# A third picked tile in layers 2 and 3 of a graph network on one core

## Chip, core and metric

The kernel runs on one of the eight cores of one Trainium2 chip. The metric is device time in microseconds of one execution. Short names stand for the units: PE (TensorE matmuls; its weight loads are shown as PEld), DVE (VectorE), ACT (ScalarE), POOL (GpSimd) and SP (SyncE, which here only issues transfers).

## What is computed

A graph of N = 5000 nodes with D = 64 features and E = 165000 edges, sorted by destination. After a layer norm and an encoder, four layers of this run one after the other:

```python
m = relu(x[src] + ea) + EPS            # ea = edge_attr @ eencW + eencb, the same in all layers
logits = m * t
e = exp(logits - segment_max(logits, dst)[dst])
agg = segment_sum(m * e / segment_sum(e, dst)[dst], dst)
h = relu(ln((agg + x) @ W1 + b1)) @ W2 + b2
```

Layers 1 to 3 add h to the running x and take relu(ln(x)) as the next layer's input. A last stage (another layer norm, a weighted sum over edges by source, written as scatters with accumulation) follows.

## The kernel before

**Windows.** The edge list is cut in two halves, h = 0 and 1, that lie on partitions 0 to 63 and 64 to 127 once features are on partitions. A layer goes through 52 full windows of 2 x 1536 edges (FULLW = 52, K = 12 columns of 128 edges for each half) and four of half the size (LAST). Buffers are double, indexed b. The full windows are in a hardware loop of two windows a turn, and every engine has its own program for it; the order on each engine is the order of the text below.

**The gather x[src].** POOL issues one indirect DMA for each column and half (L826, from the node table h_tab in DRAM into xg): 24 a window in layer 0. In later layers some (column, half) pairs, called tiles here, are not gathered but picked by PE: `is_hot` leaves out the tiles with 2*(K-1-k)+h < HOT[l]. With HOT = [0, 2, 2, 2] these are both halves of column 11, and 22 gathers remain in layers 1 to 3. A window's gathers go out only when DVE has copied its index list into idx (L1159), which DVE does at the start of the window two before, once ACT has finished zl of that window (l_ok).

**Picking a tile.** A one-hot matrix of 125 x (40 x 128) fp8 values (`hot[n]`) says which node each of the 128 edges wants. `select` (L910 to L918) multiplies it with `hb`, the node table split into three bf16 parts side by side (192 columns), in 40 matmuls that add up in a PSUM bank. ACT copies the sums to hx (L1066, one copy for each pair of tiles: ROUNDS), and PE's `forward` adds the three parts into the window's PSUM (L893). The matrices of both tiles are made in layer 0, one comparison on DVE each (L1203, `make_hot`; MADE_IN says in which layer tile n is made), stored by SP to DRAM (`keep_hot`, L734), and loaded again in layers 1 to 3 (`load_hot`, L729). There is one buffer for each tile, so SP issues the load for window w when PE has finished that tile's matmuls of window w-1, tile after tile.

**A window on the engines, layers 1 to 3.** PE: forward of window w+1 (L901 transposes of the gathered tiles, L893), back of w (L933, 24 transposes), then select of w+2. ACT: for w+1 keep (L1028), u (L1031, three pieces) and zl (L1035, signals l_ok), then emptying of w to st_all (L1050, six), exponentials (L1057, L1058), the features of w+2 into PSUM (L1042), and the picked rows of w+2 (L1066). DVE: L1159, then four scans (L1166, L1167, L1180, L1184) with small steps between, then make_hot where the layer makes matrices. SP: features ea (L662) and run penalties rp (L651) of w+2, load_hot of w+2, store of st_all (L706), zeros (L711), keep_hot and load_columns (L718) of a made tile.

**Between the layers.** POOL gathers the last row of each node's run from sums (L851), and PE, ACT and DVE do the node part in 11 chunks. As a chunk of h_cur is ready (h_ok), SP stores it to h_tab (`store_nodes`, L714). The next layer's gathers wait for all 11 (tab_out). After layer 3 nothing gathers from these rows; the last stage writes h_tab anew (L1465).

Of the kernel before, what the change touches and what calls it, by code (L numbers as in the profile page):

```python
# [32 lines left out]
N, D, E, L = 5000, 64, 165000, 4  # L33
# [29 lines left out]
NCH = len(NODE_SIZES)  # L63
# [6 lines left out]
XT = 5  # L70
ROWS = EPAD // W
ROWS_REAL = E // W
HOT = [0, 2, 2, 2]
MADE_IN = [0, 0]
NHOT = len(MADE_IN)
ROUNDS = [-(-n // 2) for n in HOT]
PN = N // NT
# [15 lines left out]
def gnn(nc, x, src, dst, edge_attr, edge_weight, encW, encb, eencW, eencb, W1, b1, lnG, lnB, W2, b2,  # L93
# [18 lines left out]
    with ExitStack() as whole:  # L112
# [3 lines left out]
        def sem(name):  # L116
            return whole.enter_context(nc.semaphore(name))
# [372 lines left out]
        with ExitStack() as c:  # L490
# [53 lines left out]
            with ExitStack() as lists_room:  # L544
# [26 lines left out]
            x_ok, xsum_ok, xroot_ok, ha_ok, h_ok, tab_out = (  # L571
                sem(n) for n in ("x_ok", "xsum_ok", "xroot_ok", "ha_ok", "h_ok", "tab_out"))
# [14 lines left out]
            FULL_PAIRS = FULLW // 2  # L587
            SPLIT = [l + 1 < L and HOT[l + 1] > 0 for l in range(L)]
            SPLIT_ROOMS = [(rx.rearrange("p (t d) -> p t d", d=D), slice(0, W // D)),
                           (turn.rearrange("p (t d) -> p t d", d=D), slice(W // D, NT))]  # L590

            def xg_window(l, gr):
                return 16 * (2 * GT - (HOT[l] if gr == NG - 1 else 0))

# [6 lines left out]
            def is_hot(l, k, h, gt):  # L601
                return gt == GT and 2 * (K - 1 - k) + h < HOT[l]

            def made(l):
                return [n for n in range(NHOT) if MADE_IN[n] == l]

# [3 lines left out]
            def in_count(l, w):  # L610
                return 16 * (FULLW * sum(HOT[0:l]) + HOT[l] * (w + 1))

# [3 lines left out]
            def ps_count(l, w, n):  # L616
                return FULLW * sum(HOT[0:l]) + HOT[l] * w + n + 1

# [13 lines left out]
            with nc.Block() as block:  # L632
                @block.sync
                def _(sp):
# [8 lines left out]
                    def keep_features(g, b, gt=GT):  # L643
                        sp.wait_ge(zenc_sb, NG * (g + 1))
                        sp.dma_start(feat_v[g, :, :, 0:gt * P], at[b][:, :, 0:gt * P]).then_inc(feat_out[b], 16)
# [8 lines left out]
                    def load(g, w, b, first):  # L654
                        sp.wait_ge(z_ps, NG * g + NG - NG * 2 + Z0)
                        if first:
                            for h in range(2):
                                piece = bass.ds(h * HALF + w * W, W)
                                sp.dma_start(ea[b][:, h, :, :], edge_attr[piece, :].rearrange("(p k) f -> p k f", k=K)
                                             ).then_inc(ea_in[b], 16)  # L660
                        else:
                            sp.dma_start(turned[b][:, :, :], feat_v[w]).then_inc(ea_in[b], 16)  # L662
                        load_penalties(g, w, b)
# [32 lines left out]
                    def store_small(g, s, b):  # L696
                        sp.wait_ge(back_sb, BU * (g + 1) + BS0)
                        begin = FULLW * W + s * W // 2
                        sp.dma_start(halves[:, begin:begin + W // 2, :].rearrange("h (p k) c -> p h (k c)", k=K // 2),
                                     st[b][:, :, 0:K // 2, :].rearrange("p h k c -> p h (k c)")).then_inc(st_out[b], 16)  # L700
# [3 lines left out]
                    def store(g, w, b):  # L704
                        sp.wait_ge(back_sb, BU * (g + 1) + BS0)
                        sp.dma_start(sums_v[w], st[b].rearrange("p h k c -> p h (k c)")).then_inc(st_out[b], 16)  # L706
# [3 lines left out]
                    def clear(g):  # L710
                        sp.dma_start(head_pieces[g], zeros[:, :]).then_inc(heads_zero, 16)  # L711
# [5 lines left out]
                    def load_columns(n, w, b):  # L717
                        sp.dma_start(hot_srcB[n][b][:, :], hot_rows[n // 2, n % 2, w].partition_broadcast(P)  # L718
                                     ).then_inc(hot_src_in[b], 16)
# [3 lines left out]
                    def load_hot(l, w):  # L723
                        for n in range(HOT[l]):
                            if isinstance(w, int) and w == 0 and n == 0:
                                sp.wait_ge(hot_out, out_count(l, 0))
                            if not (isinstance(w, int) and w == 0):
                                sp.wait_ge(hot_ps, ps_count(l, w - 1, n))
                            sp.dma_start(hot_words[n][0:PN, :], hot_tab[n][w]).then_inc(hot_in, 16)  # L729

                    def keep_hot(l, w, b, more):
                        for j, n in enumerate(made(l)):
                            sp.wait_ge(hot_made, made_count(l, w, j))
                            sp.dma_start(hot_tab[n][w], hot_words[n][0:PN, :]).then_inc(hot_out, 16)  # L734
                            if more:
                                load_columns(n, w + 2, b)
# [17 lines left out]
                    def layer(l, first):  # L754
                        for n in made(l):
                            for b in range(2):
                                load_columns(n, b, b)
                        for w in range(2):
                            load_hot(l, w)
                        with sp.Fori(0, FULL_PAIRS - 1) as i:  # L760
                            for b in range(2):
                                load(l * LW + 2 * i + 2 + b, 2 * i + 2 + b, b, first)
                                if first:
                                    keep_features(2 * i + b, b)
                                load_hot(l, 2 * i + 2 + b)
                                store(l * LW + 2 * i + b, 2 * i + b, b)
                                clear(l * NW + 2 * i + b)
                                keep_hot(l, 2 * i + b, b, True)
                        for b in range(2):
                            load_small(l * LW + FULLW + b, b, b, first)  # L770
                            if first:
                                keep_features(FULLW - 2 + b, b)
                            store(l * LW + FULLW - 2 + b, FULLW - 2 + b, b)
                            clear(l * NW + FULLW - 2 + b)
                            keep_hot(l, FULLW - 2 + b, b, False)
                        for b in range(2):
                            load_small(l * LW + FULLW + 2 + b, 2 + b, b, first)
                            if first:
                                keep_features(FULLW + b, b, GT // 2)
                            store_small(l * LW + FULLW + b, b, b)  # L780
                            clear(l * NW + FULLW + b)
                        for b in range(2):
                            if first:
                                keep_features(FULLW + 2 + b, b, GT // 2)
                            store_small(l * LW + FULLW + 2 + b, 2 + b, b)
                        for b in range(2):
                            sp.wait_ge(st_out[b], 16 * PAIRS * (l + 1) + 32)
                        sp.dma_start(pold.rearrange("p a d -> p (a d)"), sums[bass.ds(last, 1), :]).then_inc(pold_in, 16)
                        sp.dma_start(hrow[:, :], h_tab[bass.ds(split, 1), :]).then_inc(pold_in, 16)
                        sp.wait_ge(patch_v, 3 * l + 3)  # L790
                        sp.dma_start(h_tab[bass.ds(split, 1), :], hnew[:, :]).then_inc(patched, 16)
                        sp.wait_ge(patched, 32 * l + 16)
                        sp.dma_start(h_cur[:, bass.ds(split_t, 1), :], h_tab.rearrange("(p t) d -> p t d", t=NT)
                                     [:, bass.ds(split_t, 1), :]).then_inc(patched, 16)
                        for b in range(2):
                            sp.wait_ge(feat_out[b], 16 * PAIRS + FT0)
                            load((l + 1) * LW + b, b, b, False)
                        for k in range(NCH):
                            sp.wait_ge(h_ok, NCH * l + k + 1)
                            store_nodes(k)  # L800

                    for l in range(L):
                        layer(l, l == 0)
                    sp.wait_ge(tab_out, 16 * NCH * L + 16)
                    sp.wait_ge(out_lists, 16 * 6)
                    sp.wait_ge(out_tabs, 16 * (2 + ACCS))
                    sp.wait_ge(heads_zero, 16 * L * NW)
# [1038 lines left out]
```

## Time and profile before

| | |
|---|---|
| median of 3 runs | 11808.61 us (11800.38 to 11816.48) |
| the profiled execution, its own time | 11828.1 us |
| its span in the profile | 11826.3 us |
| PE busy | 5802.2 us (49%), 31762 matmuls |
| weight loads | 4077.1 us (34%) |
| DVE busy | 6551.7 us (55%) |
| ACT busy | 3327.1 us (28%) |
| POOL busy | 6522.0 us (55%) |
| HBM read, written | 806.66 MB, 546.46 MB |

The span is what the records of the instructions cover, from the first to the last. All times of rows and of the text are counted from its start, and they come from this one execution; the three runs of the table are others. A busy share is a sum over stages that differ: layers 0 to 3 take roughly the first 9800 us, the last stage the rest.

### The profile page before, as it was taken

How to read it: one execution, taken by the hardware profiler on the slowest of the kernel's cores; microseconds unless marked ns; L12 is line 12 of the kernel's file. 1: busy time of each engine (PE TensorE's matmuls, PEld its weight loads, DVE VectorE, ACT ScalarE, POOL GpSimd, SP SyncE). 2: the span in 40 equal slices, each digit the busy share in tenths (PEclk: the TensorE clock that was granted, in tenths of full speed). 3: DMA queues.
4: the chain of work that ended last, by engine and by line, in shares of the span. 5: the costliest groups of instructions: out<-in, count | busy, mean ns of one | idle time of the engine just before them, and what ended most of it. 6: DMA issues, size and time to landing. Idle time of an engine off the chain costs nothing. (4 is left out here: it accounts for less than half of the span.)

```text
span 11826.3 us, 107787 instructions
## 1 busy us (share of the span) xinstructions
PE 5802.2 (49%) x31762; PEld 4077.1 (34%) x31762; DVE 6551.7 (55%) x8055; ACT 3327.1 (28%) x4948; POOL 6522.0 (55%) x6157
## 2 busy tenths in 40 slices
PE   2333333343444444444444444444444447888887
PEld 2222222232333333333333333333333334444443
DVE  5666666664444444544444445444444457998897
ACT  1333333342333333333333333333223232111110
POOL 5455455535444444454544444544444446888887
PEclk6666666666666666666666666666666668999998
DMA  5344344333333333333333333333333334555555
GB/s 155 125 137 138 123 140 132 130 109 103 118 117 117 117 117 117 102 97 116 119 118 118 117 118 106 95 117 118 117 117 117 117 112 94 99 97 99 96 94 86
DMA packets 840467, 1354.58 MB, mean 115 GB/s; under 512 B 499934, under 2 KB 556476, under 8 KB 838730
## 3 DMA queue, kind: packets, MB, share of 16 engines
q1 hardware_dynamic: 523832, 1135.94, 27.5%
q0 software_dynamic: 312640, 214.30, 12.9%
q10 hardware_dynamic: 3916, 3.40, 0.1%
q8 instruction: 36, 0.59, 0.0%
q14 instruction: 43, 0.35, 0.0%
HBM read 806.66 MB, written 546.46 MB: 114 GB/s over the span
## 5 line engine op out<-in xcount | busy, mean ns | idle before, releaser
L826 POOL DMA_INDIRECT xg<-h_tab,idx x4656 | 4461.7, 958 | 4370.0 <-DVE idx L1159 2909.3
L917 PE MATMUL turn<-hb,hot 125*128 125x192 bf16 x12480 | 1872.5, 295 | 3018.0 <-issue 2977.7
L917 PEld LDWEIGHTS turn<-hb,hot 125*128 125x128 fp8e4 x12480 | 1310.6, 114 | 3571.7 <-issue 3536.0
L1159 DVE COPY idx<-idx_full 128x24 int32 x208 | 36.6, 176 | 3526.7 <-ACT zl L1035 3526.7
L933 PE MATMUL turn<-ident,sums 128*128 128x128 f32 x5184 | 1073.7, 375 | 1533.8 <-ACT st_all L1050 1140.4
L1524 POOL DMA_INDIRECT acc<-vm,tgt x1026 | 1602.9, 1562 | 341.2 <-issue 288.1
L933 PEld LDWEIGHTS turn<-ident,sums 128*128 128x128 f32 x5184 | 878.0, 222 | 1676.3 <-ACT st_all L1050 1243.6
L1066 ACT ACTIVATE hx<-turn 128x384 bf16<-128x384 f32 x156 | 76.4, 490 | 3600.9 <-PE turn L917 3553.1
L1050 ACT ACTIVATE st_all<-turn 128x512 f32<-128x512 f32 (+1 forms) x1344 | 752.3, 577 | 698.7 <-PE turn L933 321.0
L1166 DVE TENSOR_TENSOR_SCAN rx<-rp,carry,zl 128x1536 f32<-128x1536 bf16 (+1 forms) x224 | 739.9, 3303 | 360.1 <-ACT zl L1035 343.1
L1597 PE MATMUL zl<-spreadz,lo_hot 128*128 128x512 f32 x1620 | 765.5, 609 | 95.2 <-DVE spreadz L1773 95.2
L1773 DVE TENSOR_TENSOR spreadz<-turn,hi_hot 128x2560 f32<-128x2560 f32 x270 | 762.6, 2825 | 51.7 <-ACT gh L1658 10.6
L1031 ACT ACTIVATE u<-zl,attrB 128x512 f32<-128x512 f32 (+1 forms) x672 | 659.8, 1104 | 413.6 <-remote 330.7
L1180 DVE TENSOR_TENSOR_SCAN sums<-keep,start,rx 128x1536 f32<-128x1536 bf16 (+1 forms) x224 | 739.0, 3299 | 30.2 <-DVE start L1178 0.5
L1184 DVE TENSOR_TENSOR_SCAN sums<-keep,start,rx 128x1536 f32<-128x1536 bf16 (+1 forms) x224 | 739.0, 3299 | 7.8
L1203 DVE TENSOR_TENSOR hot<-rx,hot_src 128x5120 fp8e4<-128x5120 f32 x104 | 566.2, 5486 | 315.7 <-issue 182.3
L1167 DVE TENSOR_TENSOR_SCAN segmax<-rp,rx 128x1536 f32<-128x1536 bf16 (+1 forms) x224 | 725.6, 3239 | 7.6
L901 PE MATMUL zl<-ident,xg 128*128 128x128 f32 x2436 | 459.9, 341 | 133.8 <-ACT zl L1042 52.4
L1597 PE MATMUL rx<-spreadz,lo_hot 128*128 128x512 f32 x1080 | 507.5, 592 | 0.0
L882 PE MATMUL zl<-at,attrW 128*128 128x512 f32 x336 | 250.9, 882 | 444.5 <-ACT at L1022 250.3
L901 PEld LDWEIGHTS zl<-ident,xg 128*128 128x128 f32 x2436 | 377.7, 183 | 211.3 <-issue 106.0
L1597 PEld LDWEIGHTS zl<-spreadz,lo_hot 128*128 128x128 f32 x1620 | 296.0, 196 | 408.5 <-issue 269.4
(277 smaller groups left out, 7413.2 us busy)
## 6 DMA issues: line engine op xcount, KB each, us to landing
sums<-st_all SPq DMA_DIRECT2D x208, 1536.0 KB
hot<-hot_tab SPq DMA_DIRECT2D x312, 625.0 KB
ea<-feat SPq DMA_DIRECT2D x158, 768.0 KB
srcB<-src_flat SPq DMA_DIRECT2D x108, 768.0 KB
rp<-run_pen SPq DMA_DIRECT2D x210, 384.2 KB
xg<-h_tab,idx POOLq DMA_INDIRECT x4656
hot_tab<-hot SPq DMA_DIRECT2D x104, 625.0 KB
run_head<-zeros SPq DMA_DIRECT2D x216, 192.0 KB
```

The lines of the kernel that those rows point to most:

```text
L826: g_.indirect_dma_start(xg[b][:, k, h, :], None, h_tab[:, :], bass.IndirectOffsetOnAxis(ap=idx[b][:, h, k:k + 1] if small is None else idx ...
L901: ins = pe.matmul(ps[gr][rows, (k - gr * gt) * P:(k - gr * gt + 1) * P], xg[b][:, k, halves[0]:halves[-1] + 1, :].rearrange("p h d -> p (h ...
L917: ins = pe.matmul(picked[:, :, n % 2, :], hot[n][0:PN, t_, :], hb[0:PN, t_, :, :], start=t_ == 0, stop=t_ == NT - 1, skip_group_check=True)
L933: ins = pe.transpose(ps[6 + (b + r) % 2][:, j * P:(j + 1) * P], sum_v[:, gr * gt + j, :], ident[:, :])
L1050: a.activation(st[b].rearrange("p h k c -> p k h c")[:, gr * gt:(gr + 1) * gt, :, s_ * D:(s_ + 1) * D], ps[6 + (b + r) % 2][:, 0:gt * P].r ...
L1166: link(v.tensor_tensor_scan(rx[:, 0:width], rp[b][:, 0:width], zl[:, 0:width], carry[:, 0:1], ALU.min, ALU.max))
L1167: v.tensor_tensor_scan(segmax[:, 0:width][:, ::-1], rp[b][:, 1:width + 1][:, ::-1], rx[:, 0:width][:, ::-1], -BIG, ALU.min, ALU.max).then_ ...
L1180: v.tensor_tensor_scan(den[b][:, 0:width], keep[b][:, 0:width], rx[:, 0:width], start2[:, 0:1], ALU.mult, ALU.add).then_inc(den_ok, 1)
L1184: v.tensor_tensor_scan(num[b][:, 0:width], keep[b][:, 0:width], rx[:, 0:width], start2[:, 1:2], ALU.mult, ALU.add).then_inc(sums_ok, 1)
L1524: g_.indirect_dma_start(acc[i][:, :], bass.IndirectOffsetOnAxis(ap=tgt[b][:, t_:t_ + 1], axis=0), vm[b][:, t_, :], None, compute_op=ALU.ad ...
L1597: ins = pe.matmul(bank[:, :], lo_hot[b][:, n, :], z[:, part * 512:(part + 1) * 512], start=False, stop=True, skip_group_check=True)
L1773: v.tensor_tensor(spreadz[(XT * b + n) % 2][:, :, :], rows_bank[2][:, at_:at_ + D].unsqueeze(1).broadcast_to([P, NT, D]), hi_hot[b][:, n, ...
```

## The change

In layers 2 and 3 a third tile is picked: column 10 of half 0. Its gather goes away there, and PE, ACT and SP treat tile n = 2 as they do the other two; it is alone in a second round of `picked`, in the other PSUM bank. Its matrices are made in layer 1, by `make_hot` on DVE with `keep_hot` and `load_columns` on SP; layer 1 itself still picks two. The lists that are prepared at the start hold one more column for it. The node table after the last layer is no longer stored: SP waits for h_ok there instead of issuing the eleven stores.

```diff
-HOT = [0, 2, 2, 2]
-MADE_IN = [0, 0]
+HOT = [0, 2, 3, 3]
+MADE_IN = [0, 0, 1]
...
-                        for k in range(NCH):
+                        for k in range(NCH if l + 1 < L else 0):
                             sp.wait_ge(h_ok, NCH * l + k + 1)
                             store_nodes(k)
...
-                    sp.wait_ge(tab_out, 16 * NCH * L + 16)
+                    sp.wait_ge(tab_out, 16 * NCH * (L - 1) + 16)
+                    sp.wait_ge(h_ok, NCH * L)
```

## Rows read from the trace of the kernel before

**Rows 1.** The page: the span, and busy time of each engine.
```profile
span 11826.3 us, 107787 instructions
...
PE 5802.2 (49%) x31762; PEld 4077.1 (34%) x31762; DVE 6551.7 (55%) x8055; ACT 3327.1 (28%) x4948; POOL 6522.0 (55%) x6157
```
**Rows 2.** The page's groups: operation, count | busy us, mean ns | idle before, releaser.
```profile
L826 POOL DMA_INDIRECT xg<-h_tab,idx x4656 | 4461.7, 958 | 4370.0 <-DVE idx L1159 2909.3
...
L1203 DVE TENSOR_TENSOR hot<-rx,hot_src 128x5120 fp8e4<-128x5120 f32 x104 | 566.2, 5486 | 315.7 <-issue 182.3
```
**Rows 3.** Line 1159 in 5200 to 7210 and 7600 to 9600: ns min/median/max, first and last start.
```profile
L1159 DVE COPY idx<-idx_full x47: 177/178/179, 5229.3 to 7171.5; 128x24 int32 x47
...
L1159 DVE COPY idx<-idx_full x48: 177/178/179, 7603.4 to 9588.2; 128x24 int32 x48
```
**Rows 4.** Waits of 5200 to 7200: who for whom, us in total, times, longest.
```profile
DVE idx L1159 <- ACT zl L1035: 1056.1, 47, 23.1
POOL xg L826 <- DVE idx L1159: 696.8, 47, 15.4
```
**Rows 5.** Timeline of POOL: start, us, what; first and last of 22 gathers.
```profile
6032.43 0.95 POOL L826 DMA_INDIRECT xg<-h_tab,idx  x1 [14.05 <-DVE idx L1159]
...
6058.84 0.95 POOL L826 DMA_INDIRECT xg<-h_tab,idx  x1 [0.30 <-issue]
```
**Rows 6.** Timeline of PE, 6034 to 6070: the picking of one window.
```profile
6035.31 3.96 PE L917 MATMUL turn<-hb,hot 125*128 125x192 bf16 x46
6039.49 0.24 PE L917 MATMUL turn<-hb,hot 125*128 125x192 bf16 x1 [0.23 <-issue]
...
6063.67 2.90 PE L917 MATMUL turn<-hb,hot 125*128 125x192 bf16 x17 [0.36 <-issue]
```
**Rows 7.** Timeline of ACT behind it.
```profile
6066.61 0.49 ACT L1066 ACTIVATE hx<-turn 128x384 bf16<-128x384 f32 x1 [23.60 <-PE turn L917]
...
6071.52 1.63 ACT L1035 ACTIVATE zl<-u,tcur 128x1536 f32<-128x1536 f32 x1
```
**Rows 8.** Timeline of DVE: line 1159 of this window and of the next.
```profile
6031.26 0.18 DVE L1159 COPY idx<-idx_full 128x24 int32 x1 [21.68 <-ACT zl L1035]
...
6073.32 0.18 DVE L1159 COPY idx<-idx_full 128x24 int32 x1 [22.34 <-ACT zl L1035]
```
**Rows 9.** Stretches: length, busy (count) of each engine, PEclk, DMA share, GB/s.
```profile
6056.00:6063.00 7.00, 1.30 (x5) 0.42 (x5) 0.00 (x0) 0.00 (x0) 2.88 (x4) 0.50 0.11 19
...
6063.70:6069.40 5.70, 5.70 (x35) 5.05 (x36) 0.00 (x0) 2.78 (x3) 0.00 (x0) 0.50 0.26 88
6069.50:6072.80 3.30, 1.07 (x9) 0.88 (x7) 0.00 (x0) 3.27 (x4) 0.00 (x0) 1.00 0.32 133
```
**Rows 10.** Timelines: three pickings behind their slow stretch, one stretch's last gather.
```profile
5107.85 6.97 PE L917 MATMUL turn<-hb,hot 125*128 125x192 bf16 x48 [1.09 <-issue]
...
7226.31 5.61 PE L917 MATMUL turn<-hb,hot 125*128 125x192 bf16 x46 [0.49 <-issue]
...
7483.16 5.50 PE L917 MATMUL turn<-hb,hot 125*128 125x192 bf16 x48 [0.36 <-issue]
...
7223.03 0.96 POOL L826 DMA_INDIRECT xg<-h_tab,idx_last  x1 [0.30 <-issue]
```
**Rows 11.** Timeline of SP: the loads of the hot matrices of one window.
```profile
6063.90 2.98 SPq L729 DMA_DIRECT2D hot<-hot_tab  x2
```
**Rows 12.** Timeline of DVE in layer 1: idle time before line 1159.
```profile
4034.28 0.18 DVE L1159 COPY idx<-idx_full 128x24 int32 x1 [22.66 <-ACT zl L1035]
```
**Rows 13.** Timelines of SP and ACT: the end of layer 3's node part.
```profile
9785.40 8.04 SPq L714 DMA_DIRECT2D h_tab<-h_cur  x5
9795.89 1.17 SPq L1451 DMA_DIRECT2D run<-run_pen  x2
...
9792.76 0.31 ACT L1135 ACTIVATE h_cur<-h_cur 128x128 f32<-128x128 f32 x1 [0.76 <-DVE h_cur L1360]
```
**Rows 14.** The page's DMA queues: packets, MB, share of 16 engines.
```profile
q8 instruction: 36, 0.59, 0.0%
```

## The prediction

> **What bounds the kernel now.** I read the page first for its sum: 11826.3 us, in which no engine works over 55% of the time [rows 1]. The page's chain puts names to a small part of the span only, so I went on to the groups of instructions by line [rows 2] and to one line that runs once in each window, the copy of the next index list (L1159). In layer 2 it runs from 5229.3 to 7171.5 us in 46 steps, in layer 3 from 7603.4 to 9588.2 in 47 [rows 3]: 42.2 us a window in both. This is the cycle that the change alters, in 2 x 52 = 104 windows.
>
> The waits of layer 2 show a ring: POOL's gathers wait for the copy on DVE, the copy for ACT's zl [rows 4]. So I followed one turn in the timelines. The copy at 6031.26 [rows 8] lets the gathers go: the first at 6032.43, the 22nd at 6058.84 [rows 5], which is 21 steps of 1.258 us, though an instruction's own busy time is 0.96 us [rows 2]. PE starts its 80 selecting matmuls (L917, two tiles of 40) at 6035.31 and does 46 of them at 0.082 us each ((3.96 - 0.25) / 45). Then it nearly stops: the next starts at 6039.49, and until 6063.67 only 17 more run, each about 1.4 us after the last, with weight load and matmul 0.70 us apart. The idle time has no releaser but "issue". From 6063.67 the last 17 go at 0.158 us each, 2.9 us with the tail of the last [rows 6]. ACT's copy of the picked rows follows at 6066.61, then keep, u and zl until 6073.1 [rows 7], and DVE's copy at 6073.32 closes the ring after 42.06 us [rows 8].
>
> The slow stretch isn't the granted clock: that is at its lower level, 0.5 of 2.4 GHz, in 6056 to 6063 with 5 matmuls in 7 us, and at the same level just behind with 35 in 5.7 us [rows 9]. It goes with the gathers: it ends 4.83 us after the last is issued. In the last full window of the layer, with 12 gathers behind the small lists (the last at 7223.03), it ends at 7226.31, 3.28 us after, with 46 matmuls still to come [rows 10]. I read it so: while POOL gathers, PE can run ahead by some 46 pairs of weight load and matmul, and then goes at the slow pace until the gathers are done. What the resource is the trace doesn't show; the sum only needs that it ends with the gathers.
>
> So a window is: copy to first gather 1.1, 21 steps of gathers 26.4, 4.8 to the end of the slow stretch, 2.9 for the matmuls that are left, and 6.7 for forward and ACT up to the copy: 42.
>
> **The change part by part.**
>
> **One gather fewer (104 windows).** A step of 1.26 us; and as the stretch ends 4.83 us after 22 gathers but 3.28 after 12, each gather also moves it by (4.83 - 3.28) / 10 = 0.15 us. I take 1.4 us off a window, bounds 1.26 and 1.42.
>
> **40 more matmuls (104 windows).** The run-ahead of 46 is full already, and the slow stretch is now 1.4 us shorter, about one pair less. So all 40, and 1 more, are left when it ends: 17 + 41 = 58 instead of 17. What 58 cost I take from the three places where 46 to 48 were left: 6.97 us for 48, 5.61 for 46, 5.50 for 48 [rows 10], a mean of 6.0 for 47 in which the clock rises on the way (at 6069.5 here it is at 2.4 GHz, after 5.8 us of work [rows 9]). The 11 beyond cost 0.9 us at the full clock (0.082) or 1.7 at half (0.158). I take 7.2, which is 4.3 more than the 2.9 of now. The bounds: 58 at 0.082 and a tail make 5.0 (2.1 more), 58 at 0.158 make 9.4 (6.5 more).
>
> **Copy and spreading of the third tile.** ACT copies the first two tiles while PE picks the third, then 192 columns in place of 384 (0.49 us now [rows 7]): 0.1 us less on the path. Nine small matmuls (L893) take the place of six, and the lone half of column 10 becomes a plain matmul; PE's forward is off the path there, since ACT is busy from the hx copy to the end of zl, 6.6 us without a gap [rows 7]. If PE's forward were late, zl would wait for u's third piece; I put nothing, and at most 0.5 us a window in the bound.
>
> **Third load of hot matrices.** SP waits for the end of each tile's matmuls and issues there; it stands at 6063.90 and about 6066.6 for two [rows 11]. They move at 133 GB/s with 0.32 of the DMA engines [rows 9], so 640 KB take 4.8 us and the third is down about 17 us after the slow stretch ends, when the next selection starts 11 us after the last, about 18. The margin is 1 us. If it is missed, the selection starts late but not its end: the run-ahead fills in 4 us of a stretch of 28. Nothing. What SP has queued behind (store of sums, zeros, next ea and rp) waits for ACT's emptying anyway, 12 us after the last load is issued.
>
> **Net of a steady window:** -1.4 + 4.3 - 0.1 = +2.8 us; times 104 = +291. Bounds per window: -1.42 + 2.1 - 0.1 = +0.6 (+60) and -1.26 + 6.5 = +5.3 (+550).
>
> **Starts of layers 2 and 3.** Windows 0 and 1 are picked before the loop under 44 gathers on end. There the picking of 48 left at 7483.16 is behind the stretch already [rows 10]. 80 more matmuls at 0.082 to 0.158 are 6.6 to 12.6 us, less 2.5 for two gathers, and part of it is hidden: +6 a layer, +12.
>
> **Making the third matrix in layer 1.** DVE: one comparison of 5.49 us a window [rows 2]. It stands behind a window's last scan, and DVE is idle there for 22.66 us until ACT's zl [rows 12]; no one waits for it but SP's store, which comes a window later. If that cover were gone it would be 5.5 x 52 = 286 us. The store (640 KB) and the reload of a column join SP's queue behind clear, in front of ea and rp, and delay these by about 2 us; ea is used a whole window later. The burst falls 15 us or more before the last gather. Nothing; bound 0 to +26.
>
> **Last layer's rows not stored.** Eleven stores go. SP issues the last of the final five by 9793.44 and the next stage's first transfer at 9795.89, and ACT's last relu ends at 9793.07 [rows 13]. The landing of the last store is what is saved: -2 us (bounds -2.5, 0). The others lie beside the node stage.
>
> **Sum:** 291 + 12 - 2 = +301 on the profiled execution (span 11826.3, its own time 11828.1): 12129. The median of the three runs is 19.5 us below that time, so 11808.6 + 301 = 12110.
>
> [...]
>
> **The rivals.** (A) **The third tile is free**: the run-ahead or the slow pace isn't a limit on the number, and the 40 fit beneath the gathers. Then a window loses 1.4 us and the copy 0.1: 11809 - 156 - 2 = 11651. It decides if the slow stretch lets 40 more pairs through in 22.8 us, at 0.4 us a pair; for it speaks that I can't name the resource, against it that the stretch has the same pace in every view, 1.4 us a pair. (B) **All at half clock**: PE's grant doesn't rise in the longer run of matmuls; +5.3 a window, 12370. Against it the 46 left at 7226.31, done in 5.61 us [rows 10]. (C) **The slow stretch ends with the issue of the last matmuls**, not with the gathers (17 left could be the depth of a queue). Then 40 more pairs at 1.4 us are 56 us a window, near 17600. Against it the 46 and 48 left in rows 10. [...] (E) The making in layer 1 loses its cover: 12400. That the change doesn't do what it says I see no room for: the counts of gathers follow from the list alone.
>
> **How the numbers follow.** Forecast 0.66, around 12110, between 11870 and 12380 by its bounds; A 0.11 (11651); B 0.15, at the top of the range; C 0.02; D 0.03; E 0.03. The range 11870 to 12380 leaves out A, C and most of E: 0.15. A measurement of this kernel tells 0.2% (24 us) from no change. A makes faster 0.11; the low bound of the forecast could come within 0.2%, 0.03; slower 0.86.
>
> **What would show it.** L1159 about 45.0 us apart in layers 2 and 3, 42.2 still in layer 1; gathers 21 a window, 25.2 us from first to last; about 58 of 120 selecting matmuls behind the slow stretch, taking near 7.2 us; L1203 x156 with no new wait; hot loads x3 and PE's wait for them still under 1 us; the first transfer of the last stage 2 us nearer to ACT's last relu. Wrong would be: windows under 42 us (A), the stretch longer than 24 us (C), matmuls left at 0.158 throughout (B), or a layer 1 over 42.7 us a window (E).

## The result, and the profile after

The kernel after takes **12094.5 us** (median of four runs, 12077.7 to 12102.7) where the kernel before takes 11807.3 (four runs, 11800.4 to 11816.5): ratio 1.0241, 95% interval 1.0223 to 1.0259. It is slower by 287 us. The forecast was 12110 in a range of 11870 to 12380, slower with a chance of 0.86. The profiled executions differ by 273.9 us in their spans. Lines of the kernel after are one higher than those of before from L806 on, so L826 is L827 here.

The page after: span and engines, the instruction queue, and the groups that answer to [rows 1, 2, 14].

```profile
span 12100.2 us, 118433 instructions
...
PE 6108.3 (50%) x36338; PEld 4384.7 (36%) x36338; DVE 6849.4 (57%) x8160; ACT 3354.9 (28%) x5052; POOL 6422.6 (53%) x6053
...
q8 instruction: 39, 0.64, 0.0%
...
L827 POOL DMA_INDIRECT xg<-h_tab,idx x4552 | 4363.3, 959 | 4731.8 <-DVE idx L1160 3265.8
...
L1204 DVE TENSOR_TENSOR hot<-rx,hot_src 128x5120 fp8e4<-128x5120 f32 x156 | 851.8, 5488 | 336.3 <-issue 200.4
```

POOL is busy 99 us less than before and its gathers wait 362 us more. What the engines do in sum says nothing of why; the copy that runs once a window does. Its instructions in layers 1, 2 and 3 (min/median/max, first and last start), to be held against [rows 3]:

```profile
L1160 DVE COPY idx<-idx_full x46: 178/178/180, 2944.0 to 4864.9; 128x24 int32 x46
...
L1160 DVE COPY idx<-idx_full x46: 178/178/179, 5269.9 to 7267.2; 128x24 int32 x46
...
L1160 DVE COPY idx<-idx_full x48: 178/178/179, 7772.2 to 9858.3; 128x24 int32 x48
```

That is 1920.9 / 45 = 42.69 us a window in layer 1, 1997.3 / 45 = 44.38 in layer 2 and 2086.1 / 47 = 44.39 in layer 3, where all three had 42.2. From the first to the last copy of a layer, layer 2 is 118.4 us longer than before, layer 3 120.5 and layer 1 18.5; the ways from layer to layer change by -1.6 and +6.9, what lies ahead of layer 1's first copy by +10.5, and what lies behind layer 3's last by +0.7. These add up to the 273.9.

One window of layer 2 on PE: the selecting matmuls ahead of the slow stretch, one pair in it, those behind it, then forward (compare [rows 6]).

```profile
6029.30 4.03 PE L918 MATMUL turn<-hb,hot 125*128 125x192 bf16 x45 [0.45 <-DMA hot<-hot_tab]
...
6053.15 0.32 PE L918 MATMUL turn<-hb,hot 125*128 125x192 bf16 x1 [1.11 <-issue]
...
6055.95 6.66 PE L918 MATMUL turn<-hb,hot 125*128 125x192 bf16 x59 [0.36 <-issue]
6062.44 1.04 PE L902 MATMUL zl<-ident,xg 128*128 128x128 f32 x8
```

The same window on POOL (first and last of 21 gathers), ACT (both copies of picked rows), SP (the three loads) and DVE (the copies of this window and the next), against [rows 5, 7, 8, 11]:

```profile
6025.93 0.95 POOL L827 DMA_INDIRECT xg<-h_tab,idx  x1 [17.97 <-DVE idx L1160]
...
6051.11 0.95 POOL L827 DMA_INDIRECT xg<-h_tab,idx  x1 [0.30 <-issue]
```

```profile
6059.20 0.49 ACT L1067 ACTIVATE hx<-turn 128x384 bf16<-128x384 f32 x1 [22.69 <-PE turn L918]
6062.64 0.33 ACT L1067 ACTIVATE hx<-turn 128x192 bf16<-128x192 f32 x1 [2.95 <-PE turn L918]
```

```profile
6056.19 6.71 SPq L729 DMA_DIRECT2D hot<-hot_tab  x3
```

```profile
6024.77 0.18 DVE L1160 COPY idx<-idx_full 128x24 int32 x1 [24.31 <-ACT zl L1036]
...
6069.34 0.18 DVE L1160 COPY idx<-idx_full 128x24 int32 x1 [24.84 <-ACT zl L1036]
```

And the granted clock while the matmuls that are left run (stretches, columns as in [rows 9]):

```profile
6056.00:6059.00 3.00, 3.00 (x20) 2.76 (x21) 0.00 (x0) 0.00 (x0) 0.00 (x0) 0.50 0.19 43
6059.00:6062.40 3.40, 3.40 (x42) 3.37 (x40) 0.00 (x0) 0.49 (x1) 0.00 (x0) 0.95 0.32 134
```

The ring is the same and closes after 44.57 us. The gathers span 25.18 us instead of 26.41. The stretch ends 4.84 us after the last one begins, at 6055.95, with **59 matmuls** still to run, where before 17 were left; they hold ACT's last copy of picked rows, and so keep, u, zl and the next copy on DVE, until 6062.6. In the first 3.0 us 20 matmuls run at 0.50 of the full clock, in the next 3.4 us 42 at 0.95. I averaged windows 4 to 49 of each layer over the whole trace (start to start, so without the tail of the last matmul):

| a window, mean | before, layers 2 and 3 | after, layers 2 and 3 | after, layer 1 |
|---|---|---|---|
| copy to copy, us | 42.2 | 44.4 | 42.7 |
| pairs ahead of the slow stretch | 47.5 | 46.8 | 46.9 |
| pairs in it | 14.2 | 13.8 | 11.7 |
| pairs left behind it, and us | 18.3, 2.72 | 59.4, 6.43 | 21.5, 3.19 |
| first to last gather, us | 26.44 | 25.19 | 26.45 |
| last gather to the stretch's end, us | 4.87 | 4.74 | 4.89 |

### The profile page after: what moved, and what is told of

Read it like the earlier page. It is cut to its first block and busy times, and to the rows that moved or that the text cites. A ratio compares the mean times of both kernels' runs of the same rounds, so it can differ in the third digit from the quotient of the medians.

```text
span 12100.2 us, 118433 instructions
## 1 busy us (share of the span) xinstructions
PE 6108.3 (50%) x36338; PEld 4384.7 (36%) x36338; DVE 6849.4 (57%) x8160; ACT 3354.9 (28%) x5052; POOL 6422.6 (53%) x6053
## 5 line engine op out<-in xcount | busy, mean ns | idle before, releaser
L827 POOL DMA_INDIRECT xg<-h_tab,idx x4552 | 4363.3, 959 | 4731.8 <-DVE idx L1160 3265.8
L918 PE MATMUL turn<-hb,hot 125*128 125x192 bf16 x16640 | 2173.3, 281 | 3042.3 <-issue 2920.2
L918 PEld LDWEIGHTS turn<-hb,hot 125*128 125x128 fp8e4 x16640 | 1647.2, 110 | 3568.7 <-issue 3529.4
L1067 ACT ACTIVATE hx<-turn 128x384 bf16<-128x384 f32 (+1 forms) x260 | 110.8, 426 | 3947.0 <-PE turn L918 3799.5
L1204 DVE TENSOR_TENSOR hot<-rx,hot_src 128x5120 fp8e4<-128x5120 f32 x156 | 851.8, 5488 | 336.3 <-issue 200.4
L902 PE MATMUL zl<-ident,xg 128*128 128x128 f32 x2540 | 419.4, 306 | 93.6 <-ACT zl L1043 45.3
L876 PE MATMUL turn<-ident,ea 128*64 128x128 f32 x2592 | 263.7, 381 | 287.8 <-ACT at L1023 194.8
```

What stands on the lines that cost most here:

```text
L827: g_.indirect_dma_start(xg[b][:, k, h, :], None, h_tab[:, :], bass.IndirectOffsetOnAxis(ap=idx[b][:, h, k:k + 1] if small is None else idx ...
L918: ins = pe.matmul(picked[:, :, n % 2, :], hot[n][0:PN, t_, :], hb[0:PN, t_, :, :], start=t_ == 0, stop=t_ == NT - 1, skip_group_check=True)
L1204: v.tensor_tensor(hot[n][:, :, :], rx[:, 0:NT].unsqueeze(2).broadcast_to([P, NT, P]), hot_srcB[n][b].unsqueeze(1).broadcast_to([P, NT, P]) ...
```

## The experiments

Each ratio is to the kernel before on the same chip. The two halves, the one tile and the making alone ran on one chip (kernel before: 11787.5 us); for the others its time is given where the plain times are compared.

**Two halves of the change, each alone.** First the gather goes and no tile takes its place, so column 10 of half 0 gets no x[src] in layers 2 and 3 (`not_gathered` is `is_hot` with GONE[l] for HOT[l]):

```diff
+GONE = [0, 2, 3, 3]
-                                if is_hot(l, k, h, gt):
+                                if not_gathered(l, k, h, gt):
                                     continue
```

> The change's saving alone: column 10 of half 0 is not gathered in layers 2 and 3 and nothing is picked for it, so that half column's x[src] is left out of the computation there. Leftover theory: the stretch ends 1.4 us sooner, one pair more is left (0.15): -1.25 a window, 104 windows, -130, about 11675. Rival, the slow stretch is a fixed number of matmuls and not tied to the gathers: no change in the window, 11807.

It took 11658.8 us, 0.9890 [0.9874, 0.9907]. Its line 1163 in layer 2:

```profile
L1163 DVE COPY idx<-idx_full x38: 177/178/179, 5326.6 to 6831.8; 128x24 int32 x38
```

That is 40.7 us a window (40.9 in layer 3), and the count left stays near 18: the gather alone is worth 1.3 to 1.5 us a window where it leaves PE's load as it was. Then the other half: the third tile is picked and its gather is issued all the same, into a place that nobody reads (GONE = [0, 2, 2, 2] on the kernel after).

> The change's cost alone: third tile picked in layers 2 and 3, its gather issued as before (the row is fetched and not used). Leftover theory: 44.4 us (as changed) + 1.4 - 0.15 = 45.6 us a window, 58 pairs left behind the stretch, about 12094 + 130 = 12225. If the matmuls were hidden by the longer gathers, 44.4 or less a window and 12094 or below.

12241.7 us, 1.0383 [1.0365, 1.0402]. One of its windows, behind the slow stretch:

```profile
6070.80 6.68 PE L922 MATMUL turn<-hb,hot 125*128 125x192 bf16 x60 [0.36 <-issue]
```

Windows of layers 2 and 3 are 46.1 us apart, with 58 pairs left in 6.7 us on average. So both halves work in the way that the prediction had them: -1.4 and +3.9 make +2.5, against 2.2 measured. The 0.3 us between agree with the price of the pairs left, 6.75 us here and 6.43 in the change, where the clock rises sooner (more on it below).

**One tile fewer.** If what is left behind the stretch is what costs, the kernel before pays too, for its second tile (HOT = [0, 1, 1, 1], MADE_IN = [0]).

> The other way from the change: layers 1 to 3 pick one tile (40 matmuls) and gather 23. Theory of the leftover (the slow stretch of PE ends with the gathers, 4.9 us after the last; only matmuls that are left then lengthen a window): 40 matmuls fit in the run-ahead of 47, none is left. A window is 1.2 to the first gather, 22 steps of 1.258 = 27.7, 5.0 to the end of the stretch, 0 left, 6.9 to the next index copy = 40.8 us in place of 42.2; 156 windows: -220, about 11590 us. Rival, the number of matmuls doesn't matter (case A of the prediction): one gather more is +1.4 a window, 12030. Rival, end of issue ends the stretch: no slow stretch at all, below 40 us a window.

11695.8 us, 0.9918 [0.9902, 0.9935]: faster, by less than half of what I expected. The windows aren't why: one of layers 1 to 3 takes 40.5 us, 0.3 less than the sum said, and no selecting matmul is left. The copy of the picked rows still comes late. PE is done with all 40 at 6007.2; ACT gets to copy at 6032.90, 5.1 us after the last gather begins (PE, POOL, ACT):

```profile
6003.05 4.19 PE L917 MATMUL turn<-hb,hot 125*128 125x192 bf16 x40
```

```profile
6027.82 0.96 POOL L826 DMA_INDIRECT xg<-h_tab,idx  x1 [0.30 <-issue]
```

```profile
6032.90 0.33 ACT L1066 ACTIVATE hx<-turn 128x192 bf16<-128x192 f32 x1 [22.23 <-remote]
```

What was missing is lost where nothing is picked: layer 0 takes 140 us more, here before (first line) and with one tile (second).

```profile
L1159 DVE COPY idx<-idx_full x52: 168/170/173, 180.4 to 2467.7; 128x24 int32 x52
```

```profile
L1159 DVE COPY idx<-idx_full x52: 169/170/278, 180.6 to 2608.0; 128x24 int32 x52
```

**One tile picked, both made.** The only difference from that run is one matrix more made in layer 0 (HOT = [0, 1, 1, 1], MADE_IN = [0, 0]).

> One tile picked in layers 1 to 3, as in the run with one picked tile, but both tiles' matrices are made in layer 0, as before. That run's windows in layers 1 to 3 were 40.5 us apart (before 42.2), and gave 60 to 70 us per layer; but its layer 0, which made one matrix instead of two, took 140 us longer from its first index copy to its last (2427 against 2287 us), alternating between windows of 66 and 26 us. If it is the one making less that put layer 0 into that rhythm, this kernel has layer 0 back at about 2287 us and takes 11696 - 140 = 11555 us. If layer 0 is slow for another reason (chance, or the kernel's size), it stays near 11695 us.

11565.8 us, 0.9785 [0.9768, 0.9801] (kernel before here: 11816.8), and layer 0 is back:

```profile
L1159 DVE COPY idx<-idx_full x52: 169/170/173, 180.8 to 2461.2; 128x24 int32 x52
```

So one picked tile is better than two by 2.1% and three are worse by 2.4%. Why layer 0 falls into windows of some 70 and 26 us by turns when it makes less (53 and 36 are common in the kernel before), no run here tells.

**The length of the slow stretch.** Is it set by the gathers, or a number of its own? GONE = [0, 2, 7, 7] leaves 17 gathers a window in layers 2 and 3, and five parts of x[src] out of the sum.

> As the kernel with 21 gathers and two picked tiles, but with 17 gathers per window in layers 2 and 3 (the x[src] part of both halves of columns 9 and 10 and more of the last group is left out of the sum; TensorE's picks are those of before). Theory (TensorE's slow stretch ends a fixed 4.7 to 4.9 us after the last gather begins, wherever that is): the stretch is 24.0 - 5 x 1.258 = 17.7 us, some 10 pairs run in it, 23 are left instead of 18 (3.4 us instead of 2.7), and a window takes 42.1 - 6.3 + 0.7 = 36.5 us: 11787 - 104 x 5.6 = 11205 us where the kernel before takes 11787. Rival: the stretch has a length of its own or comes from TensorE's own count of instructions; then the windows stay near 42 us or drop by less than 2 us, 11600 to 11790 us.

11172.7 us, 0.9418 [0.9404, 0.9433] (kernel before here: 11865.0). In layer 2 the copies are 1546.2 / 43 = 36.0 us apart. One window's last gather, and the matmuls behind its stretch:

```profile
L1163 DVE COPY idx<-idx_full x44: 178/178/180, 5302.6 to 6848.8; 128x24 int32 x44
```

```profile
6007.49 0.95 POOL L830 DMA_INDIRECT xg<-h_tab,idx  x1 [0.30 <-issue]
```

```profile
6011.81 3.84 PE L921 MATMUL turn<-hb,hot 125*128 125x192 bf16 x23 [0.38 <-issue]
```

The stretch is 17.4 us on average instead of 24.1, ends 4.2 us after the last gather begins, and 22.5 pairs are left (expected 23). It follows the gathers. The time of 17 gathers is even a bit better than expected, since the end moves in by 0.7 us more than the five steps, as the prediction had taken from the window with 12 [rows 10].

**Making in layer 1 alone.** MADE_IN = [0, 0, 1] with HOT = [0, 2, 2, 2]: the third tile's matrices are made and stored in layer 1 and read nowhere.

> The third tile's matrices are made and stored in layer 1 as in the change, and never used; two tiles are picked everywhere. The prediction had 0 for it. Its trace showed layer 1 at 42.7 us a window against 42.2, so if that is the making it is +0.46 x 52 = +24, 11831 us, with fewer pairs (12 instead of 14) in the slow stretch. If it was chance of that execution: within 5 us of before.

11812.9 us, 1.0027 [1.0015, 1.0038]. Layer 1's windows are 42.6 us apart, layer 2's 42.1: half a microsecond a window, some 25 us, which the prediction had at nothing. Two runs test its first two suspects. With 5 of 125 partitions stored:

> As the kernel that makes the third tile's matrices in layer 1 and picks it nowhere (that one took 25 us longer than the kernel before on this chip, and its layer 1 windows were 42.60 us apart where they are 42.2 us before), but of each third matrix only 5 of 125 partitions are stored; VectorE's comparison is as long as it was. If the store's 640 KB among the other transfers is what costs 0.4 us per window, layer 1 is back at 42.2 us and the time at 11790 us; if it is VectorE's comparison or the wait for its columns, the windows stay at 42.6 us and the time at 11813 us.

11843.6 us, 1.0020 [1.0010, 1.0030]; 42.7 against 42.2 us. With the comparison and the store each cut to 5 of 40 columns:

> As the kernel that makes the third tile's matrices in layer 1 and picks it nowhere, but VectorE's comparison and the store each cover 5 of the 40 columns of a tile. With the full comparison layer 1's windows are 42.6 us apart, also with only 5 of 125 partitions stored, so the store is not what costs. If it is the 5.5 us comparison, in whose time TensorE's pairs come every 2.1 to 2.8 us instead of every 1.4 us, the windows are back at 42.2 us and the time is that of the kernel before (11790 to 11817 us, by the chip). If it is the step's waits and small copies, they stay at 42.6 us, 24 us above it.

11878.6 us, 1.0015 [1.0005, 1.0024]; 42.8 against 42.45 us. Most of the difference is there in both (0.5 and 0.4 us), so neither the 640 KB nor the 5.49 us is the main cause; whether the shorter comparison takes a tenth of a us off, one trace each can't tell. Then only the queue's part, without any step of the making on DVE in the windows:

> As the kernel that makes the third tile's matrices in layer 1 and picks it nowhere, but in layer 1 VectorE makes nothing (the third tile's matrices are left at zero, stored each window, and read nowhere), so the queue's store and its load of the columns go out each window without waiting for VectorE. With a store of 5 of 125 partitions, and with a comparison of 5 of 40 columns too, layer 1's windows stayed 0.4 to 0.5 us above those of layers 2 and 3 (42.68 against 42.15 to 42.20, and 42.83 against 42.45 to 42.48 us). Theory: the wait is what costs: VectorE's step comes late in the window, the queue stands before it, and features and penalties of the next window are issued some 10 us later; then layer 1 here is within 0.1 us of layers 2 and 3 and the time that of the kernel before. Rival: the two more transfers per window cost by themselves; then layer 1 stays 0.4 to 0.5 us above, 22 us above the kernel before.

11819.3 us, 1.0021 [1.0009, 1.0032] (kernel before here: 11793.2). Its copies in layer 1 and in layer 2:

```profile
L1162 DVE COPY idx<-idx_full x45: 177/178/179, 2969.9 to 4832.5; 128x24 int32 x45
...
L1162 DVE COPY idx<-idx_full x45: 178/178/179, 5308.7 to 7162.8; 128x24 int32 x45
```

42.33 against 42.14 us: less than half of the difference is left, so part of it goes with DVE's step and the queue's wait for it, and part with the transfers; the time itself can't tell this from the full making. What the trace shows is where it lands: in layer 1 after, only 11.7 pairs get through the slow stretch, where the same layer has 14.5 before, and 3 more are left. By what way a step on DVE or a small transfer slows PE's pairs stays open.

**No last store.** The end of the queue of the kernel after, on the kernel before.

> The kernel before with one part of the change alone: the last layer's node rows are not stored, and the queue waits for the node steps instead. The prediction put this at 2 us off the end (the last store's way to its landing, after the node steps). So 11785 us beside 11787 of the kernel before, no difference that rounds can show; in the trace the distance from the last index copy to the end of the span should be about 2 us shorter than the 2212.9 us of before. Rival: the stores before it have landed under the node steps and the end is set by something else, then the distance stays, and only the bytes written fall.

11820.3 us, 0.9995 [0.9984, 1.0006] (kernel before here: 11816.8), no difference, as it must be for 2 us. The distance from the last index copy to the end is 2212.4 us instead of 2212.9.

**The order of PE's work.** If the pairs that are left cost their time, some of them should be run where nothing gathers. In the kernel before PE is idle between its back transposes while ACT is busy with zl, for 3.15 us in the window of layer 2 followed above:

```profile
6073.72 3.81 PE L933 MATMUL turn<-ident,sums 128*128 128x128 f32 x16 [3.15 <-ACT st_all L1050]
```

So the first tile is picked ahead of the transposes, straight behind forward; ACT copies it ahead of the evictions, into one bank while the transposes begin in the other, and each tile's load has its own semaphore.

```diff
                                 forward(g0 + w + 1, i + b, l, 1 - b)
-                                back(g0 + w, b, ahead=rounds_done(l, w + 2) if HOT[l] else 0)
-                                select(g0 + w + 2, w + 2, l, b)
+                                if HOT[l]:
+                                    select(g0 + w + 2, w + 2, l, b, [0])
+                                back(g0 + w, b, ahead=rounds_done(l, w + 2) + 1 if HOT[l] else 0)
+                                select(g0 + w + 2, w + 2, l, b, range(1, HOT[l]))
```

> The kernel before, two tiles picked, with the first tile's 40 matmuls issued straight behind the forward matmuls of the window before, ahead of the back transposes, where TensorE is idle for 3.1 us and no gather is running; its part of the PSUM copy goes ahead of the evictions. The second tile stays where both were. The work is the same. Theory of the prediction (what is left behind the slow stretch is on the ring: 18 pairs, 2.7 us in each of 156 windows): only 40 pairs start with the gathers, fewer than the 47 that go before the slow stretch, so none is left, the windows come 39.5 us apart, and the time is 11787 - 421 = 11366 us; if the back transposes, some 1.5 us later, push the gathers or the forward matmuls back by as much, 11600 us. Rival: the matmuls left are not on the ring and the forward matmuls wait for gathered rows that land late; then the windows stay at 42.2 us and the time at 11790 us or above.

Its six runs took 11377, 11377, 11384, 11837, 11844 and 12313 us; the ratio of the fastest three is 0.9628 [0.9608, 0.9647]. The profiled one took 11844 and has both rhythms. Layers 1, 2 and 3:

```profile
L1165 DVE COPY idx<-idx_full x46: 177/178/406, 2920.7 to 4683.2; 128x24 int32 x46
...
L1165 DVE COPY idx<-idx_full x45: 177/178/180, 5178.4 to 7320.2; 128x24 int32 x45
...
L1165 DVE COPY idx<-idx_full x46: 177/178/180, 7804.1 to 9564.8; 128x24 int32 x46
```

Layers 1 and 3 have 39.2 and 39.1 us a window, layer 2 has 48.7: 9.5 x 49 windows are the step of 465 us between the times. In layer 2 the first tile's load is late, its matmuls run while POOL gathers, and the copy that the transposes wait for comes only after the gathers (PE, then ACT):

```profile
6018.15 4.98 PE L919 MATMUL turn<-hb,hot 125*128 125x192 bf16 x40 [18.52 <-DMA hot<-hot_tab]
...
6038.57 4.42 PE L935 MATMUL turn<-ident,sums 128*128 128x128 f32 x20 [14.91 <-ACT hx L1070]
```

```profile
6038.19 0.33 ACT L1070 ACTIVATE hx<-turn 128x192 bf16<-128x192 f32 x1 [34.41 <-remote]
```

I read it so: that makes the evictions, the store and with them the next load late again, and the long rhythm feeds itself. So the first tile's load got two buffers by turns (the third tile's, free here) and a place ahead of features and penalties in the queue:

```diff
+                                load_first(l, 2 * i + 2 + b, b)
                                 load(l * LW + 2 * i + 2 + b, 2 * i + 2 + b, b, first)
...
-                                ins = pe.matmul(picked[:, :, n % 2, :], hot[n][0:PN, t_, :],
+                                ins = pe.matmul(picked[:, :, n % 2, :], (hot[n] if n else hot_even[b])[0:PN, t_, :],
```

> The kernel with the first tile's matmuls ahead of the back transposes had two rhythms, each kept through a whole layer: 39.1 us per window (its layers 1 and 3, in the profiled run) and 48.7 us (its layer 2), so that its times fell on 11377, 11840 and 12313 us. In the long rhythm TensorE waits 18.5 us for the first tile's load, which is issued behind the sums store, the features and the penalties, and picks while the gathers run. Here that load has two buffers by turns and is issued a step earlier in the queue, ahead of features and penalties. Theory: the late load keeps the long rhythm alive, so now every layer is at 39.1 us and all times lie at 11377 us, within 0.3%. Rival: any late start, however it comes, keeps itself up through the late signals of TensorE (picked copy, evictions, store), then the times still fall on steps of some 465 us.

**11424.8 us**, five runs from 11417.9 to 11426.2 (kernel before here: 11865.0), ratio 0.9628 [0.9615, 0.9641], the ratio of the short rhythm: in these five runs the long one is gone, and the kernel beats the one before with the same arithmetic. It changes two things at once, the buffers and the place in the queue; which of them is needed isn't shown. One window on PE:

```profile
6028.88 5.27 PE L936 MATMUL turn<-hb,hot 125*128 125x192 bf16 x40
6033.99 4.28 PE L952 MATMUL turn<-ident,sums 128*128 128x128 f32 x24
6038.39 3.46 PE L936 MATMUL turn<-hb,hot 125*128 125x192 bf16 x40
```

Forty matmuls ahead of the transposes, forty behind them, none left; 39.3 us a window in layers 1 to 3, 2.9 less than before, of which the pairs left were 2.7.

## Why the prediction was right, point by point

**The ring and the slow stretch.** Right. The windows of layers 2 and 3 are 44.4 us apart, and the stretch ends 4.74 us after 21 gathers, 4.87 after 22, 4.2 after 17. With all 40 matmuls of a window through before the stretch, the ring still turns on the gathers.

**The gather: -1.4 us.** Right: 25.19 for 26.44 us, and 0.13 us from the stretch's end; alone it gave 1.1% of the kernel's time.

**40 more matmuls: +4.3 us.** The count was right (59.4 for a forecast of 58), the price was the term that was mis-sized: +3.7 us (6.43 for 2.72), inside its bounds. The trace tells the clock as a share of full speed, 0.50 and then 1.00 [rows 9]; no run shows the 2.4 GHz that the forecast calls it, and the price stands on the 0.158 and 0.082 us a matmul of rows 6 and the three places of rows 10. I took the clock's rise at 5.8 us after the stretch's end from one window, and it was one of the latest: over 46 windows of layer 2 before, it rises 2.7 to 5.9 us after that end, 4.3 on average. After the change it rises 2.9 to 4.4 us after, 3.3 to 3.4 on average. With the gather kept it rises after 4.2 us, and there the term is +4.0 us (6.75 for 58 pairs). The 21 gathers alone don't explain the sooner rise, since with 21 and only 18 pairs left it comes after 3.9 us; what does isn't shown. Over 104 windows the 0.6 us are 62 us.

**Copy, third load.** The rest of the window is some 0.2 us shorter (-0.1 forecast). The third load is down just in time: PE waits for it in 17 windows of layer 2, at most 0.9 us, ahead of a stretch that swallows it.

**Starts of layers, +12 us.** The first copies to the last are 18.6 us longer than 2.16 us x 51 in both layers together, and the ways between layers 5.3 us longer: some 24.

**Making in layer 1: nothing.** Wrong by some 25 us, within the bound of 26. The step that failed is "no one waits for it but SP's store": no wait appears, DVE is idle for 16.3 us behind it, but PE gets fewer pairs through the stretch.

**The last store: -2 us.** The next stage's first transfer is issued at 10067.74, 1.6 us after the start of ACT's last relu at 10066.12; before it was 3.1 us [rows 13]. In the time it is lost.

**The sum.** Steady windows came to 2.16 x 102 = 220 us where the forecast had 291 for 104. Layer 1 (18.5 us), the starts (24) and 10.5 us ahead of layer 1's first copy gave 53 where the forecast had 10. The 10.5 us may be chance or a part of the making, whose first loads of columns stand there: the way from layer 0's last copy to layer 1's first takes 255 to 266 us in the traces that make a tile in layer 1 and 247 to 258 in those of two picked tiles in the old order that don't. Misses of opposite sign left 27 us between the 12129 forecast for the profiled execution and its 12101.9, and 16 between 12110 and the median; that it is so near is in part luck. The upper end of the range, 12380, leaves out the 0.5 us a window that the spreading was given; with it, it would be some 12430. Nothing came of that.

**The rivals.** A (a free third tile) fell with the 59 left; B (half clock throughout) with 0.95 granted at 6059; C with the end of the stretch at 59 pairs, not at the last. E (the making without its cover, 5.5 us in each window of layer 1) came to a tenth of that. D (0.03, the longer loop fetched anew) no run shows: from 5270 to 7267, over 45 windows of layer 2 after, the trace lists packets of q0 and q1 alone and none of an instruction queue, and q8 has 39 in the whole run where it had 36 [rows 14].

## What to carry to other kernels

Work that was moved here from a slow engine to an idle one was cheap only up to where it ends before the thing that holds the ring; 40 pairs beyond that cost 3.7 us a window. Count the instructions that fit ahead of that point (here some 47 pairs and 14 more), and price only those beyond it. Then look at the order on the idle engine before its amount: the same 80 matmuls cost 2.7 us a window behind the transposes and nothing when half of them run ahead. Look at the load that feeds the work moved ahead as well: with the load left as it was, one layer of three kept a slower rhythm to its end, 48.7 us a window for 39.2, and with two buffers and an earlier place in the queue all three had 39.3.

## What the hardware did that I had not expected

**PE's signals are late while POOL gathers, not only its instructions.** In the run with one tile, the records of PE's 40 matmuls end at 6007.2 and ACT's copy, for which only their signal was missing, began at 6032.90; with the tile picked ahead and late, 6023.1 and 6038.19. In each case ACT moves 4.6 to 5.1 us after the last gather begins, as the slow stretch does (the last gather of the second case starts at 6033.59). The trace also records when a semaphore is updated, and there the delay lies: at 6032.87 and 6038.17 in these two, 0.03 and 0.02 us ahead of ACT. The kernel before has it in every window. In 45 windows of its layer 2 the first tile's last matmul ends 24.5 us ahead of its update on average, and the update comes 4.6 to 5.1 us after the last gather begins; for the second tile, done behind the stretch, it is 0.01 us. So the first tile's last matmul, recorded as ended early in a gathering window, is known to others only 4.6 to 5.1 us after the last gather begins. Whether it was done by then (ends of matmuls are modelled) or only its signal was held, and whether the two engines share something, the trace doesn't tell.

**With a making step in the window PE gets fewer pairs through the stretch**, 11.8 to 11.9 in layer 1 instead of 14.3 to 14.7 in the later layers of the three runs above, in 24 us, with 40 columns compared or 5 and with 125 partitions stored or 5; by what way is open. **And less work in layer 0 made it 140 us slower**, by a rhythm of windows of some 70 and 26 us that appears with one matrix made and not with two.
